# A four-layer graph network on one core: where x is normalised during the load, where W3's sign is taken, and when the last turned quarter of adj is widened

## The reference

```
h = relu(layernorm(x)); x = x + D (adj.T) D (h @ W0) + b0          D = diag(colsum(adj) ** -0.5)
h = relu(layernorm(x)); inc = adj + mask / sqrt(count of mask per row); x = x + (inc @ h) / rowsum(inc)
h = relu(layernorm(x)); 4 heads: softmax(leaky_relu(s_i + d_j) + adj) @ (h @ W2_head), mean over heads; x = x + that
h = relu(layernorm(x)); x = x + relu(adj @ (step(h) @ sign(W3).T))
```

## Time and profile before

| | us, or as named |
|---|---|
| median of three runs | 708.93 |
| the profiled execution | 708.1 |
| its span in the profile | 706.3 |
| TensorE busy in it | 685.5 (97%) |
| VectorE, ScalarE, GpSimd busy | 619.0, 458.4, 112.2 |
| DMA in the page's 40 slices, GB/s: the load's first three; the highest of all | 337, 375, 363; 425 |
| chain of waits that ended last: share of TensorE, VectorE, ScalarE | 83%, 8%, 4% |

### The profile page before, as it was taken

The page is one execution under the profiler, slowest core; times in us unless marked ns, Lnnn a source line. Parts: engine busy times, 40 slices in busy tenths (PEclk is TensorE's granted clock), DMA queues, the critical chain, the costliest instruction groups (busy, mean ns, idle before and its releaser), DMA issues.

```text
span 706.3 us, 15923 instructions
## 1 busy us (share of the span) xinstructions
PE 685.5 (97%) x6416; PEld 585.8 (83%) x6416; DVE 619.0 (88%) x1134; ACT 458.4 (65%) x784; POOL 112.2 (16%) x146
## 2 busy tenths in 40 slices
PE   3899999999999999999999999999999999999998
PEld 3786888888888864488888888888888888888887
DVE  5998999958989968899999999999999899994672
ACT  3895158639898327975559776686865878654650
POOL 3005623321133110002100012100211000000000
PEclk9999999999999999999999999999999999999999
DMA  9996999993799967589988799998999893474391
GB/s 337 375 363 262 425 425 270 315 247 122 209 283 237 227 171 206 164 179 207 238 199 233 140 233 240 240 248 173 194 245 222 232 207 82 76 190 140 131 309 38
DMA packets 167000, 159.53 MB, mean 226 GB/s; under 512 B 115536, under 2 KB 128528, under 8 KB 160912
## 3 DMA queue, kind: packets, MB, share of 16 engines
q1 hardware_dynamic: 145568, 100.32, 53.1%
q0 software_dynamic: 19056, 41.42, 26.1%
q10 hardware_dynamic: 2304, 16.78, 5.7%
HBM read 69.86 MB, written 52.46 MB: 173 GB/s over the span
## 4 chain that ended last, share of the span: by engine, by line
PE 83%; DVE 8%; ACT 4%; issue 4%; DMA 1%; POOL 0%; SPq 0%; ACTq 0%; POOLq 0%; DVEq 0%
PE ps L843 15%; PE ps L845 15%; PE ps L844 15%; PE ps L780 6%; PE ps L890 4%; PE ps L889 4%; PE ps L678 3%; PE ps L677 3%; PE ps L676 3%; DVE arena L1260 2%; DVE arena L1343 2%; PE ps L725 1%; DMA arena<-adj_t 1%; PE ps L727 1%; PE ps L726 1%
## 5 line engine op out<-in xcount | busy, mean ns | idle before, releaser
L843 PE MATMUL ps<-arena 128*128 128x257 f16 x1024 | 279.9, 273 | 1.3 <-DVE arena L1483 1.3
L845 PE MATMUL ps<-arena 128*128 128x257 f16 x1024 | 279.4, 273 | 0.0
L844 PE MATMUL ps<-arena 128*128 128x257 f16 x1024 | 279.2, 273 | 0.0
L1176 ACT ACTIVATE arena<-arena 128x512 f16<-128x512 f32 x252 | 158.3, 628 | 97.9 <-PE ps L845 79.6
L1476 DVE SCALAR_TENSOR_TENSOR arena<-arena,w_j 128x512 f32<-128x512 f32 x256 | 190.1, 743 | 0.0
L1483 DVE TENSOR_TENSOR arena<-arena 128x512 f16<-128x512 f32 x256 | 175.7, 687 | 9.1 <-ACT arena L1176 8.8
L843 PEld LDWEIGHTS ps<-arena 128*128 128x128 f16 x1024 | 99.9, 98 | 14.3 <-ACT arena L1176 1.5
L844 PEld LDWEIGHTS ps<-arena 128*128 128x128 f16 x1024 | 100.3, 98 | 12.6
L845 PEld LDWEIGHTS ps<-arena 128*128 128x128 f16 x1024 | 99.8, 97 | 12.9
L725 PE MATMUL ps<-arena 128*128 128x257 f16 x256 | 70.3, 275 | 0.0
L727 PE MATMUL ps<-arena 128*128 128x257 f16 x256 | 69.8, 272 | 0.0
(11 more groups left out here) (149 smaller groups left out, 1061.2 us busy)
## 6 DMA issues: line engine op xcount, KB each, us to landing
adj_t<-arena POOLq DMA_DIRECT2D x32, 1024.0 KB, 7.7
arena<-in_adj_dram SPq DMA_DIRECT2D x30, 1024.0 KB, 6.0
adj_parts<-arena ACTq DMA_DIRECT2D x16, 1024.0 KB, 21.6
arena<-adj_t SPq DMA_DIRECT2D x64, 256.0 KB, 4.9
arena<-adj_t SPq DMA_DIRECT2D x10, 1024.0 KB, 6.5
x<-arena POOLq DMA_DIRECT2D x15, 512.0 KB, 6.2
arena<-u_rows SPq DMA_DIRECT2D x4, 1024.0 KB, 14.5
x<-in_x_dram SPq DMA_DIRECT2D x4, 512.0 KB, 5.6
```

Of the source, the lines that this page charges most:

```text
L843: mm(ps[:, bank, 0:DE], hi, ht_hi[:, head, j, 0:DE], start=s, stop=False)
L844: mm(ps[:, bank, 0:DE], hi, ht_lo[:, head, j, 0:DE], start=False, stop=False)
L845: ins = mm(ps[:, bank, 0:DE], lo, ht_hi[:, head, j, 0:DE], start=False, stop=e)
L1176: nc.scalar.activation(p_hi[:, j % 4, :], prob[:, j % 4, :], copy).then_inc(p_hi_done, 1)
```

## The change

In the load, x's blocks are normalised into their own rows of `hw` (which the product overwrites afterwards), so that no buffer has to come free. Of each four blocks VectorE does the first, behind pieces 0, 2, 4 and 7, and GpSimd the other three, right behind the root of that group. The matmuls that nobody reads are one behind each piece to piece 13, six behind pieces 14 to 16, and eight at the end. W3 is loaded behind piece 10; VectorE's first instruction on it stands before the wait for the column sums and the second right behind their scaling; TensorE turns it before j = 6 of layer 0's first loop, and ScalarE copies it behind the 16 `g_hi`, in front of the DMA issues for parts 2 to 5 of adj. `WIDEN_AFTER` moves n = 12 from behind group 7 to behind 6, n = 13 from 8 to 7, and n = 15 from 9 to 8, with 14 (which stays there).

```diff
-        w3_f = view(141 * KB, [DC, D], F32)
-        w3_s = view(143 * KB, [DC, D], F16)
-        h0_n = view(G0 + 2 * KB, [2, D], F32)
+        w3_f = view(G0 + 2 * KB, [DC, D], F32)
+        w3_s = view(161 * KB, [DC, D], F16)
...
+        NORM_AFTER = (0, 2, 4, 7)
...
-        WIDEN_AFTER = {0: (6,), 1: (7,), 3: (8,), 4: (9, 10), 5: (11,), 7: (12,), 8: (13, 14), 9: (15,)}
+        WIDEN_AFTER = {0: (6,), 1: (7,), 3: (8,), 4: (9, 10), 5: (11,), 6: (12,), 7: (13,), 8: (14, 15)}
...
                 load_piece(n)
+                if n == 10:
+                    sp.dma_start(w3_f, w3_d.rearrange("(c p) d -> p c d", p=P)).then_inc(w3_in, 16)
...
-            reload_rows(8)
-            sp.wait_ge(y_ps, NB)
-            sp.dma_start(w3_f, w3_d.rearrange("(c p) d -> p c d", p=P)).then_inc(w3_in, 16)
-            for t in range(9, 12):
+            for t in range(8, 12):
                 reload_rows(t)
...
                 nc.gpsimd.tensor_tensor(rstd[:, XP * p:XP * p + XP], var_eps[:, XP * p:XP * p + XP],
                                         neg_half[:, XP * p:XP * p + XP], ALU.pow).then_inc(rstd_done, 1)
+                pool.wait_ge(rstd_done, p + 1)
+                for t in range(XP * p + 1, XP * p + XP):
+                    nc.gpsimd.tensor_scalar(hw[:, t, :], x[:, t, :], mean_var[:, t, 0:1], rstd[:, t:t + 1],
+                                            ALU.subtract, ALU.mult).then_inc(pool_normed, 1)
...
             def turn_w3():
                 pe.wait_ge(w3_signed, 1)
-                pe.wait_ge(part_lo_done, 4 * len(PE_ROWS))
...
             def h0_transposes(t):
-                pe.wait_ge(normed, t + 1)
+                if t % XP == 0:
+                    pe.wait_ge(normed, t // XP + 1)
+                else:
+                    pe.wait_ge(pool_normed, t // XP * (XP - 1) + t % XP)
...
-                    unread(2)
+                    unread(1 if n < row_slot(NB - 1) + 2 else 6)
             ins.then_inc(deg_done, 1)
-            unread(6)
+            unread(8)
...
             for j in range(NB):
+                if j == 6:
+                    turn_w3()
                 pe.wait_ge(g_lo_done, j + 1)
...
-                    if g == 1 and t == NB - 1:
-                        turn_w3()
...
-            pe.wait_ge(w3_t_done, 1)
             ht_half(0)
...
+                if t == 4:
+                    act.wait_ge(w3_signed, 1)
                 nc.scalar.activation(g_hi[:, t, :], hw[:, t, :], copy,
                                      scale=dinv_in[:, t:t + 1]).then_inc(g_hi_done, 1)
+            act.wait_ge(w3_t_ps, 1)
+            nc.scalar.activation(bw_t[:, :, :].rearrange("p c d -> p (c d)"), ps16(5)[:, 0:DC * D], copy
+                                 ).then_inc(w3_t_done, 1)
             for k in range(2, 6):
                 send_nat(k)
...
             def h0_norm(t):
-                if t % XP == 0:
-                    dve.wait_ge(rstd_done, t // XP + 1)
-                if t >= 2:
-                    dve.wait_ge(h0_t_ps, t - 1)
-                v.tensor_scalar(h0_n[:, t % 2, :], x[:, t, :], mean_var[:, t, 0:1], rstd[:, t:t + 1],
+                dve.wait_ge(rstd_done, t // XP + 1)
+                v.tensor_scalar(hw[:, t, :], x[:, t, :], mean_var[:, t, 0:1], rstd[:, t:t + 1],
                                 ALU.subtract, ALU.mult).then_inc(normed, 1)
...
                 adj_low(n)
-                for t in range(NB):
-                    if row_slot(t) - 1 == n:
-                        h0_norm(t)
+                if n in NORM_AFTER:
+                    h0_norm(XP * NORM_AFTER.index(n))
+            below_w3()
             dve.wait_ge(deg_done, 1)
             v.tensor_scalar(deg[:, :], ps[:, 4, 0:NB], 2.0 ** -16, None, ALU.mult).then_inc(deg_copied, 1)
+            sign_w3()
```

More of the change, by code:

```diff
@@ L255, in gnn_stack @@
         normed = sem("normed")
+        pool_normed = sem("pool_normed")
         h0_t_done = sem("h0_t_done")
@@ L611, in turn_w3 @@
                 pe.wait_ge(w3_signed, 1)
-                pe.wait_ge(part_lo_done, 4 * len(PE_ROWS))
                 for c in range(DC):
                     for oc in range(DC):
-                        ins = nc.tensor.transpose(ps16(0)[:, (c * DC + oc) * P:(c * DC + oc + 1) * P],
+                        ins = nc.tensor.transpose(ps16(5)[:, (c * DC + oc) * P:(c * DC + oc + 1) * P],
                                                   w3_s[:, oc, c * P:(c + 1) * P], ident16[:, :])
@@ L633, in h0_transposes @@
                     ins = nc.tensor.transpose(ps[:, H0_BANK[t % 3], c * P:(c + 1) * P],
-                                              h0_n[:, t % 2, c * P:(c + 1) * P],
+                                              hw[:, t, c * P:(c + 1) * P],
                                               ident[:, :])
@@ L1048, in _ @@
                     h2_high(t - 1)
[L1049 to L1052, removed]
                 if 2 <= t and t + 5 < NB:
@@ L1231, in link, with below_w3, sign_w3 @@
                 dve.wait_ge(dv, made[0])
-            def sign_w3():
+            def below_w3():
                 dve.wait_ge(w3_in, 16)
                 link(v.tensor_scalar(w3_s, w3_f, 0.0, None, ALU.is_lt))
+            def sign_w3():
                 v.scalar_tensor_tensor(w3_s, w3_f, 0.0, w3_s, ALU.is_gt, ALU.subtract).then_inc(w3_signed, 1)
@@ L1429, in _ @@
                     w2_a(t - 12, range(HEADS))
-                if t == 13:
-                    sign_w3()
                 if t == 14:
```

## The result

The change made the kernel slower: 710.88 us median (20 runs) against 708.33 (20 runs), a ratio of 1.0040 (95% interval 1.0027 to 1.0054). Forecast were 703.8 and a range of 702.2 to 707.2, so the direction was wrong as well. The profiled execution is the slowest of its twenty, 714.14 us with a span of 712.3, 6.0 above the span of before, where the medians differ by 2.5.

What follows compares the result with a forecast made beforehand. TensorE, 83% of the chain of waits, was taken as the bound, except in the load, where VectorE's cycle sets the pace. Gains of 1.3 + 0.8 + 1.7 + 1.3 = 5.1 us gave a 703.8 us median, range 702.2 to 707.2.

Steps and rivals of the forecast that it cites:

- The load's pace: Load: each GpSimd block holds VectorE up 0.45 us, pieces about 2.65; last low part at 55.8, 3.0 us earlier.
- its sign of being wrong: Load: the prediction is wrong if a normalisation on GpSimd is over 0.8 us, or if L1260 grows.
- The rival I gave for "slower": Load: GpSimd's normalisation holds VectorE for its whole time at every piece; 711.8 us at 1.05 a block; chance 6%.
- Four or five of 0.60: Load: VectorE's waits for a buffer, four or five of 0.60 us, go away, 2.6 us.
- The load's end: Behind the last low part: unread matmuls cost 1.2 us and sign_w3 0.5, so layer 0 starts 1.3 earlier, at 60.8.
- The clock should stay up there: Load's end: TensorE's clock stays up, with six unread matmuls behind each piece.
- sign_w3's 0.5: Load's end: GpSimd's root of the first column waits for VectorE's sign_w3, 0 to 0.6 us, taken at 0.5.
- Between the layers: Layers 1 to 2: wait and W3 turning gone, 0.8 us; clock stays up, 1.7 us, the least sure step.
- The last quarter: Head products: transfer 13's high part goes 13.2 us earlier, so TensorE's 1.29 us wait goes; gain 1.3, bounds 0 and 1.5.
- group 7's sum is not ready before 487.9, so nobody waits: Head products: GpSimd's queue waiting for turned transfer 12 ahead of group 7's sum delays nobody.

Runs made afterwards that it cites:

- e13: The changed kernel with each group's root made on GpSimd one group ahead of its blocks; 1.0008 of the kernel before.
- e5: The changed kernel with VectorE normalising all 16 blocks and GpSimd making only the four roots; 0.9988 of the kernel before.
- e2: W3's part alone on the kernel before, blocks normalised by VectorE into hw's rows with every wait of before; 0.9979.
- e1: The load's part of the change alone on the kernel before, W3 and the widening as before; 1.0061.
- e8: Changed kernel, VectorE normalising all blocks, two unread matmuls behind pieces 14 to 16, low part replaced by a copy; 706.75 us once, no time of this program.

## Why the prediction was wrong

- **The load's pace: failed, and it decides.** The step was "a block's addition holds VectorE up for 0.41 to 0.47. [...] I take 0.45", with "VectorE also waits for a root that queues behind GpSimd's blocks, twice, in small pieces: 0.4". I took what a GpSimd instruction costs VectorE for what it costs GpSimd. The earlier trace rows said the other half: GpSimd waits until VectorE's instruction ends. A block is 1.22 alone and 2.93 in the median, past the 0.8 that the prediction had named as its sign of being wrong. At 22.6 us GpSimd had nine blocks to finish and not seven; the twelve kept it at work from 13 to 50 us, and the root waits were 7.5 us in place of 0.4. VectorE's low parts were held up by 0.2 in three (2.27 apart for 2.20). Load end 62.2, forecast 55.8: 6.4 us of a miss of 7.1. The rival I gave for "slower" had the wrong mechanism too: it made VectorE's low parts longer. e13 shows the right one (with the root waits gone TensorE waits for the blocks), and e5 what it costs. "Four or five of 0.60" for the buffer waits was misread too (the trace of before has three); the sum did not use it.
- The Trainium skill ("GPSIMD Engine Reference", section 4.1) calls one input roughly line rate: not here, 1.22 us for 256 columns with two operands per partition. The Trainium skill ("SBUF — State Buffer", section "Who interferes with whom") also calls the port pair that the two engines share an exclusive lock. The traces agree for GpSimd, which is blocked for one to three of VectorE's low parts; they do not for VectorE, whose low part beside a running block is 0.1 to 0.2 us longer and not the block's 1.2.
- **The load's end: right in kind, perhaps too small in size.** Forecast 1.2 for the unread matmuls; the profile has 1.1, but the medians say 1.3 to 2.4, with a fall of the clock in one profile as the likely rest, which is not shown for the medians. "The clock should stay up there" was an argument, not a row, and e5's profile has it at 0.50. sign_w3's 0.5 did not come: GpSimd's first root started at 64.69, before VectorE's instruction at 64.89, and took 0.58.
- **Between the layers: right.** 0.8 and 1.7 were forecast and found; W3's part alone 0.9979, 1.5 us, interval 0 to 2.9. The reason I gave for the clock is not shown: the stretch it was drawn from had the clock at 0.50 behind it in e2's profile, and e1 kept its wait and lost no clock. So the 1.7 came as forecast, by luck as far as these runs tell.
- **The last quarter: right at its end, wrong on the way.** "group 7's sum is not ready before 487.9, so nobody waits": GpSimd's queue waited 10.5 us for the high part, where the waits of before are 5.8 and 7.05, and the sum stood behind it. The profiled execution paid 3.4 and the clock's 1.7; the medians show neither the gain nor this loss beyond their intervals.

## What to carry to other kernels

An engine that takes work over is priced by its own duration beside its neighbour, not by what its neighbour loses to it; and what queues behind the new work on it (here four small roots) is part of the price. Matmuls that only keep the clock up go where nothing waits for the next real one. Before a transfer is moved ahead in an in-order queue, look at the slowest landing of its kind and not the usual one, for what stands behind it.

## What the runs showed of the hardware

- GpSimd's tensor_scalar on 128x256 float32, with two per-partition operands: 1.22 us alone; beside VectorE instructions with two inputs in SBUF 3.5, 4.7, once 7.56, and three of these take 6.89 us instead of 6.69. In the earlier trace rows GpSimd's additions and VectorE alternate one to one; these blocks don't get that share. Why was not tried.
- DMA into the core reached 411 to 424 GB/s in the load when slots came back early (e8), against 351: a share of 0.95 busy did not mean that it was full.
